# A self-wait on TensorE behind the first layer of each of 39 expert steps

## What is computed

```
x = x + conv_block(layernorm_over_channels(x))      # 4 dilated dynamic 3x3 branches, 3 group norms
t = tokens(x)                                        # 4096 x 128
n = layernorm(t)
top2, which = top_k(n @ gate_w.T, 2)                 # 8 experts, 2 for each token
weight = softmax(top2)
for e in range(8):
    h = gelu(n @ w1[e].T + b1[e])                    # 128 -> 512
    y = h @ w2[e].T + b2[e]                          # 512 -> 128
    t += weight[:, e] * y                            # only for tokens that chose e
```

## Time and profile before

| | us |
|---|---|
| median of 3 runs | 382.11 |
| their range | 379.77 to 383.36 |
| the profiled execution, its own time | 376.91 |
| its span (first to last instruction) | 375.1 |
| PE busy | 299.2 (80%) |
| POOL busy | 200.9 (54%) |
| DVE busy | 177.4 (47%) |
| ACT busy | 146.8 (39%) |

### The profile page before, as it was taken

One profiled execution on the slowest core, in us unless ns is written; L12 is line 12 of the kernel. 1 busy time (PEld: TensorE's weight loads), 2 busy tenths in 40 slices (PEclk: granted clock), 3 DMA queues, 4 the chain that ended last, 5 costly groups with the idle time before them and its releaser, 6 DMA issues.

```text
span 375.1 us, 4690 instructions
## 1 busy us (share of the span) xinstructions
PE 299.2 (80%) x1475; PEld 208.0 (55%) x1475; DVE 177.4 (47%) x424; ACT 146.8 (39%) x352; POOL 200.9 (54%) x193
## 2 busy tenths in 40 slices
PE   3999989868979875869894999889889598897044
PEld 1245443523426673658783887667678487675033
DVE  3653999998857895099430021102111032213077
ACT  3643121211036854386434444524524153244072
POOL 9200669777700417528375667557557556644362
PEclk9999999968998969869898999999999899999655
DMA  8000000000000246325253565346346345440395
GB/s 303 29 3 0 2 0 0 2 0 0 0 3 0 88 184 226 108 83 193 76 163 93 162 177 183 102 160 211 119 135 219 98 143 158 157 148 29 128 366 206
DMA packets 13767, 41.79 MB, mean 111 GB/s; under 512 B 3120, under 2 KB 3120, under 8 KB 13744
## 3 DMA queue, kind: packets, MB, share of 16 engines
q1 hardware_dynamic: 8640, 29.52, 23.1%
q0 software_dynamic: 4096, 8.40, 7.3%
q10 hardware_dynamic: 1008, 3.59, 2.5%
HBM read 32.05 MB, written 9.44 MB: 111 GB/s over the span
## 4 chain that ended last, share of the span: by engine, by line
PE 49%; DVE 20%; issue 7%; another core or an unknown queue 6%; POOL 5%; DMA 5%; ACT 5%; DVEq 2%; SPq 0%; POOLq 0%; ACTq 0%
PE PS L1424 15%; PE PS L1435 14%; PE PS L1271 5%; DVE PRF L871 4%; PE PS L1257 3%; PE PS L1218 3%; POOL RX L470 2%; DVE PRF L1173 2%; ACT MV L700 2%; DMA WE<-experts 2%; PE PS L1389 2%; PE PS L1413 1%; PE PS L1446 1%; DMA SCR<-expert_rows 1%
## 5 line engine op out<-in xcount | busy, mean ns | idle before, releaser
L700 ACT ACTIVATE MV<-PS,WE 128x256 f32<-128x256 f32 x156 | 61.2, 478 | 68.5 <-PE PS L1424 41.0
L1435 PE MATMUL PS<-MV,WE 128*128 128x256 f32 x312 | 78.1, 395 | 12.1 <-issue 6.7
L1424 PE MATMUL PS<-SCR,WE 128*128 (+1 forms) x312 | 79.2, 399 | 5.4 <-DMA WE<-experts 1.9
L522 POOL DMA_INDIRECT expert_rows<-RX,dsti x64 | 64.1, 1002 | 35.1 <-issue 20.7
L1435 PEld LDWEIGHTS PS<-MV,WE 128*128 128x128 f32 x312 | 60.8, 198 | 23.6 <-issue 13.5
L477 POOL TENSOR_TENSOR PRF<-PRF 128x1024 f32<-128x1024 f32 x21 | 49.5, 2361 | 40.2 <-DVE PRF L871 38.6
L1424 PEld LDWEIGHTS PS<-SCR,WE 128*128 128x128 f32 x312 | 59.0, 199 | 15.4 <-issue 7.9
L515 POOL DMA_INDIRECT RX<-token_rows,dsti x46 | 44.3, 963 | 35.7 <-issue 17.6
L1133 DVE TENSOR_SCALAR PRF<-PS,WE 128x256 f32 x30 | 14.5, 484 | 100.5 <-remote 43.6
L871 DVE TENSOR_TENSOR PRF<-RX,PS 128x512 f32<-128x512 f32 x66 | 41.7, 675 | 6.0 <-PE PS L1257 5.9
L1257 PE MATMUL PS<-FT,k 72*128 72x512 f16 x72 | 27.7, 406 | 5.1 <-DVE PRF L871 3.5
(11 more groups left out here) (240 smaller groups left out, 379.2 us busy)
## 6 DMA issues: line engine op xcount, KB each, us to landing
WE<-experts SPq DMA_DIRECT2D x39, 514.5 KB
token_rows<-SCR SPq DMA_DIRECT2D x4, 512.0 KB, 3.6
SCR<-expert_rows SPq DMA_DIRECT2D x4, 512.0 KB, 8.0
SCR<-expert_rows ACTq DMA_DIRECT2D x4, 512.0 KB, 8.3
out<-PRF SPq DMA_DIRECT2D x8, 256.0 KB, 2.1
X<-x ACTq DMA_DIRECT2D x2, 512.0 KB, 6.4
X<-x SPq DMA_DIRECT2D x2, 512.0 KB, 8.2
first_token_rows<-SCR SPq DMA_DIRECT2D x2, 512.0 KB, 2.6
```

Source lines behind the costliest of these rows:

```text
L522: nc.gpsimd.indirect_dma_start(yr, bass.IndirectOffsetOnAxis(ap=dsti[:, 1, q:q + 1].bitcast(U32), axis=0), YS[:, q % NR, :], None).then_in ...
L700: last = nc.scalar.activation(GF[:, j % 2, c * STEP:(c + 1) * STEP], first_layer(j, c), ACT.Gelu, bias=part(j, "b1")[:, c:c + 1])
L1424: last = nc.tensor.matmul(first_layer(j, c), part(j, "w1")[:, c * P:(c + 1) * P], columns, start=True, stop=True)
L1435: last = nc.tensor.matmul(second_layer(j), part(j, "w2")[:, c * C:(c + 1) * C], GF[:, j % 2, c * STEP:(c + 1) * STEP], start=(c == 0), sto ...
```

## The change

One wait is added on TensorE. Behind the 8 matmuls of the first layer of step j, whose last raises `h_done`, TensorE now waits until `h_done` has reached j + 1, that is until the signal of this layer has arrived. It then goes on with what it did before. Nothing is removed or moved, and no other engine's list changes.

```
             for c in range(HC):
                 last = nc.tensor.matmul(first_layer(j, c), part(j, "w1")[:, c * P:(c + 1) * P], columns,
                                         start=True, stop=True)
             last.then_inc(h_done, 1)
+            pe.wait_ge(h_done, j + 1)

         def output(j):
             pe.wait_ge(gelu_done, j + 1)
```

## The result

| | before | after |
|---|---|---|
| median of 5 runs, us | 382.11 | 391.55 |
| range, us | 376.98 to 383.36 | 385.56 to 393.59 |
| ratio, 95% interval | | 1.033 (1.025 to 1.041) |
| profiled execution, its own time, us | 376.91 | 385.56 |
| span, us | 375.1 | 383.8 |

The changed kernel is slower by 3.3%. I had forecast 2.4% faster. The ratio sets only the faster executions of the two kernels against each other; over all five the medians lie 9.4 us or 2.5% apart. The interval of the ratio, taken of 382 us, is 9.7 to 15.7 us. The profiled executions differ by 8.65 us, which is near the difference of the medians, so the two traces can be set against each other.

What follows compares the result with a forecast made beforehand. TensorE was taken as the bound of the expert stage, with late signals causing its idle time. From the profiled 376.9 us, less 20.1 given back, plus 16.0 for waits: 372.8, predicted as 373 us; range 366 to 400.

Steps and rivals of the forecast that it cites:

- signals of TensorE are late: Expert stage, rounds 5 to 38: 16 of 34 GELUs start late behind their first layer, 46 us in sum.
- two sorts of waits: TensorE idle time not due to signals: 1.9 us for weights, 1.2 us of "issue", taken off 19.84 us.
- two cold layers: Two layers at the lower clock behind long stalls, 3.58 and 3.64 us instead of 1.89; 3.4 us to regain.
- The price: Cost of the added wait when the signal is on time: 0.41 us a round, 16.0 us for 39 rounds.
- the hand-over from the signal to the next matmul: Behind the new wait, from signal to TensorE's next matmul: 0.14 us a round, bounds 0.05 and 0.30.
- a stop once in a round keeps signals on time: Inference that TensorE stopping behind each first layer prevents late signals, giving back 20.1 us in the expert stage.
- the slower rival: Behind first layers TensorE stops for every late signal: up to 419 us, 396 at half the lateness; chance 0.18.
- its threshold: Point where waiting out lateness makes the change a loss: more than 9 us of the 46 left.
- The first rival: Only the first layer's signal is cured; second-layer and turned-tile signals still hang: 386 us; chance 0.22.
- The pure cost: TensorE's gaps have another cause and stay, while 39 waits cost 16.0 us: 398 us; chance 0.10.
- The rival that I built on it: By the PSUM acknowledgement rule, TensorE's gaps stay and 39 waits add 16.0 us: 398 us; chance 0.10.

Runs made afterwards that it cites:

- e5: Kernel before with only the first 8 of 64 gathers and last 8 of 64 scatters left; 343.5 us, ratio 0.917 to the kernel before.
- e6: Changed kernel with only 8 of 64 gathers and 8 of 64 scatters left; 356.2 us, ratio 0.948 to the kernel before.
- e9: Changed kernel run once more without any edit; 386.2 us, ratio 1.026 to the kernel before.
- e4: Kernel before with TensorE self-waits behind both the first and the second layer of each step; 390.5 us, ratio 1.050 to the kernel before.
- e13: Kernel before with every gather and scatter replaced by a plain POOL transfer of the same size, place and waits; 341.2 us, ratio 0.908.

## Why the prediction was wrong, step by step

- **That signals of TensorE are late was right.** The trace after shows it on TensorE itself, and e5 shows the stage without it. The size was too small: I counted TensorE's idle time less two sorts of waits, and two cold layers, 20.1 us; e5 gives 30.1. The other 10.3 us are in the busy column (141.1 and 130.8): every resumed layer counts 0.17 us more to its modelled end and 0.10 us for its first weight load, and further layers ran at the lower clock.
- **The price was near.** 0.41 us predicted with 0.32 as lower bound; 0.33 measured (e5, e6). The term that was too high is the hand-over from the signal to the next matmul: 269.16 stands 0.06 us behind the layer's end, and I had taken 0.14. For 39 rounds 12.7 us and not 16.0.
- **The failed step** is the one named as the weakest: "that a stop once in a round keeps signals on time", with the 20.1 us that it was to give back. The windows show 4 to 6 us of it, all 39 rounds 1 to 2, and TensorE is idle 20.4 us in rounds 5 to 38 as before. The stop does its work in part: 16 late GELUs became 9 (12 in e9), and two stops in a round leave 2 (e4). But what is left is no longer covered. Before, a late first-layer signal cost TensorE nothing until the second layer needed its GELU; 46.5 us of lateness came down to 30 us of loss. After, 19.4 us of lateness at the first layer cost 18.9 us of idle TensorE, one to one, plus slow layers behind it. That is the slower rival, "TensorE waits out the lateness", at part of its size; its threshold, a loss once more than 9 us of the 46 are left, held: 19 were left. That is in part luck, as the 9 us are the difference of two terms that were both off.
- **Where the argument went wrong**: I took TensorE's run ahead for the cause of the late signals because they appear where it runs ahead. POOL's indirect transfers run in the same rounds, and e5 and e13 show that it takes them: TensorE runs ahead as before and nothing is late. The evidence against was in my own rows: the signal that came 4.19 us behind a TensorE that had already stopped. And the copy at 280.23 that I read as let out by TensorE's stop started 1.85 us behind the end of a run of nine transfers, as three others did.
- **The first rival** (own signal cured, others not) isn't told apart in full. In the bad round above the copy of the turned tile, raised before the first layer, came late too, and so in six of the 9; in round 18 (layer ended at 251.67) that copy was on time and only the layer's own signal was late. Both happen.
- **The pure cost** rival gives the measured time in the end, with the price of 12.7 us against 9.4 by the medians and 12.6 by the ratio, but by another way: the gaps are not the old ones that stayed, they are behind L1424 now.
- The Trainium skill's rule in "Perfetto Trace Analysis", section "Tensor Engine Instruction (MATMUL, LD_WEIGHTS)", that the signal is pushed on PSUM's acknowledgement, agrees with this kernel without its indirect transfers (34 GELUs each in e5 and e13, all 0.1 us behind the layer's modelled end) and doesn't explain what is seen with them. The rival that I built on it came closer than my forecast, though its picture of the gaps doesn't hold. The Trainium skill's advice in "VectorE: DVE Perf Modes", section "The TRN2 errata", to space dense completion signals, is given there against a deadlock; it says nothing of late signals, so it was weak support for my step, and no run here shows that the two are one thing.

What stays open: by what path indirect transfers of POOL hold back TensorE's signals, and whether it is their form, the order of the rows, the longer time that POOL spends on each, or the long runs that come of this; e13 changes all four. A version that breaks the runs of the kernel before by a pause on POOL, with the same transfers, would tell, and wasn't run. I know of no version that does the same routing with plain addresses, so none that beats both kernels was run.

## What to carry to other kernels

A wait on an engine's own signal turned a lateness that run-ahead had covered into idle time here, though it left fewer signals late, and it costs a restart in every round (0.33 us here) even when nothing is late. When consumers start late behind an engine that had finished, look first for what else runs in just those rounds, and take that away in an experiment, before changing the engine's own order. And what a lateness costs is read from the stage without it, as in e5 (30.1 us), and not from the idle time of one engine (19.8).

## What the runs showed of the hardware

- TensorE's signals, otherwise seen by a waiting engine within 0.1 us, came 0.7 to 8.9 us late in 16 of 34 rounds beside POOL's indirect DMAs, and on time beside plain DMAs of the same size from POOL (e13). It cost 28.7 us (by e13) to 30.1 us (by e5) of a 160.9 us stage. The GELU behind the bad round above is one of them; the largest in the kernel before came 8.9 us behind its layer.
- The effect is far from proportional: of the sum of 46.5 us, 12.0 are left with scatters alone and 0.7 with gathers alone.
- 14 of the 16 late ones belong to layers that ended behind five or more indirect transfers issued 0.30 us apart, and four late copies start 1.85 to 1.88 us behind the end of a run of nine.
- ScalarE's signals were on time beside them: in the same rounds TensorE started 0.05 us behind the end of a GELU that it waited for the earlier trace rows.
